# Queries of two heads in one product, moved across partitions by DMA, and the maximum's products of a pair of heads as two row tiles of 64

## The reference, cut to what matters

```
D_MODEL, H, DK, DV = (128, 16, 64, 64)
q = (x @ Wq + bq).reshape(B, S, H, DK)
k = x @ Wk + bk
v = x @ Wv + bv
scores = jnp.einsum('bshd,btd->bhst', q, k) / np.sqrt(DK)
w = jax.nn.softmax(scores, axis=-1)
out = jnp.einsum('bhst,btd->bshd', w, v).reshape(B, S, H * DV)
return out @ Wo + bo
```

## Time and profile before

| | |
|---|---|
| median of three runs | 1417.2 us (1414.25 to 1417.55) |
| the profiled execution | 1409.84 us, span 1408.0 us |
| TensorE busy | 1286.0 us, 91% of the span |
| VectorE busy | 1011.7 us, 72% |
| ScalarE busy | 708.6 us, 50% |
| products for the maximum (L1348) | 512; idle before them 34.9 us |
| reductions for the maximum (L987) | 512 of 685 ns |

### The profile page before, as it was taken

One profiled execution on the slowest core, in us unless ns is written; L12 is line 12 of the kernel. 1 busy time (PEld: TensorE's weight loads), 2 busy tenths in 40 slices (PEclk: granted clock), 3 DMA queues, 4 the chain that ended last, 5 costly groups with the idle time before them and its releaser, 6 DMA issues.

```text
span 1408.0 us, 22235 instructions
## 1 busy us (share of the span) xinstructions
PE 1286.0 (91%) x7377; PEld 760.0 (54%) x7377; DVE 1011.7 (72%) x2393; ACT 708.6 (50%) x1300; POOL 270.9 (19%) x314
## 2 busy tenths in 40 slices
PE   4569988999989998999899999999999979999997
PEld 2335435554545555555454555555655538686844
DVE  7776866578857875787668766876687747677875
ACT  3126544544464445444554445544545448677741
POOL 3033222200120012001200120012000205454630
PEclk9569998999999999999999999999999989999999
DMA  2051433000210021003000200020000246465451
GB/s 75 0 158 61 151 108 138 29 17 19 84 32 17 18 85 32 18 18 85 31 17 19 85 32 17 18 85 32 18 17 19 62 136 207 155 214 170 144 179 48
DMA packets 69299, 100.25 MB, mean 71 GB/s; under 512 B 29196, under 2 KB 45132, under 8 KB 65220
## 3 DMA queue, kind: packets, MB, share of 16 engines
q1 hardware_dynamic: 54628, 66.23, 15.2%
q0 software_dynamic: 11344, 31.64, 6.9%
q10 hardware_dynamic: 3216, 0.97, 0.3%
HBM read 59.86 MB, written 38.68 MB: 70 GB/s over the span
## 4 chain that ended last, share of the span: by engine, by line
PE 73%; DVE 16%; issue 3%; DMA 2%; ACT 2%; SPq 2%; POOL 1%; DVEq 0%; ACTq 0%; POOLq 0%
PE bank L1420 14%; PE bank L1392 8%; PE bank L1348 7%; PE bank L1431 6%; PE bank L1393 6%; PE bank L1256 5%; PE bank L1258 5%; PE bank L1257 5%; PE bank L1452 4%; DVE mneg L987 3%; PE bank L1272 2%; PE bank L1262 2%; DVE q_lm L981 2%; PE bank L1307 2%; PE bank L1289 1%
## 5 line engine op out<-in xcount | busy, mean ns | idle before, releaser
L815 ACT ACTIVATE wide<-bank 128x512 f32<-128x512 f32 x512 | 301.5, 604 | 493.3 <-PE bank L1393 483.0
L987 DVE TENSOR_REDUCE mneg<-bank 128x1 f32<-128x512 f32 x512 | 347.2, 685 | 182.2 <-PE bank L1348 176.5
L1420 PE MATMUL bank<-wide,v_w 128*32 128x512 f32 x2048 | 249.5, 605 | 0.5 <-issue 0.5
L1348 PE MATMUL bank<-k_hl,q_hh 128*128 128x512 f32 x512 | 208.0, 407 | 34.9 <-DVE mneg L987 21.7
L1392 PE MATMUL bank<-q_hh,k_hl 128*128 128x512 f32 x512 | 234.7, 458 | 1.7 <-ACT wide L815 1.4
L1393 PE MATMUL bank<-q_lm,k_h 65*128 65x512 f32 x512 | 203.6, 398 | 0.0
L1392 PEld LDWEIGHTS bank<-q_hh,k_hl 128*128 128x128 f32 x512 | 97.0, 189 | 131.1 <-issue 89.5
L614 POOL TENSOR_TENSOR rs<-rs,power 128x4 f32<-128x4 f32 x24 | 24.6, 1026 | 626.4 <-DVE rs L889 626.4
L1348 PEld LDWEIGHTS bank<-k_hl,q_hh 128*128 128x128 f32 x512 | 98.1, 192 | 72.6 <-issue 51.7
L1431 PE MATMUL bank<-wide,ones 128*32 128x512 f32 x992 | 129.1, 592 | 0.0
L684 POOL DMA_INDIRECT y_rows<-y_m,to_u x92 | 104.2, 1132 | 127.0 <-DVE y_m L1114 105.1
(11 more groups left out here) (231 smaller groups left out, 1970.4 us busy)
## 6 DMA issues: line engine op xcount, KB each, us to landing
w_t<-w_rows SPq DMA_DIRECT2D x23, 1024.0 KB
x_rows<-part_h POOLq DMA_DIRECT2D x65, 258.0 KB, 6.1
inv<-inverse_scratch SPq DMA_DIRECT2D x124, 128.0 KB, 2.9
w_rows<-w_t SPq DMA_DIRECT2D x8, 1024.0 KB, 4.9
x_m<-x_rows SPq DMA_DIRECT2D x23, 258.0 KB, 3.6
stage<-in_L_ffn_W SPq DMA_DIRECT2D x16, 256.0 KB, 5.2
yab<-y_rows POOLq DMA_DIRECT2D x8, 512.0 KB, 9.4
xin<-in_L_attn_x SPq DMA_DIRECT2D x8, 256.0 KB, 5.9
```

Of the source, the lines that this page charges most:

```text
L815: act.activation(wide[:, st.g % WIDE, :], ps, ACT.Exp, scale=SCALE1).then_inc(wide_full, 1)
L987: dve.tensor_reduce(mneg[:, (gh // 2) % 2, col:col + 1], ps[:], X, ALU.max, negate=True)\
L1348: into(("mx", gh, j), lambda ps: pe.matmul(ps[:], q_hh[:, gh % HEADS, P * j:P * j + P], k_hl[:, n % 2, :], start=True, stop=True))
L1420: pe.matmul(ps_out[0][rows, :], v_w[:, n, c, TILE * d:TILE * d + TILE], weights, start=(c == 0), stop=(c == TT - 1))
```

## The change

One product makes the queries of two heads: the weights stand once (`wq_h` of [P, H, DK]), so that the even head's query comes out on partitions 0 to 63 and the odd head's on 64 to 127. ScalarE rounds each half by itself, two activations of 64x512, and two DMAs on SyncE's queue copy each half of `q_hh` to the other 64 partitions, because `first` still wants the query in both halves. VectorE's remainders are two instructions as before, the second with its input on the upper partitions and its output on the lower. The two heads' products for a maximum are issued one behind the other, each of depth 64, with operands on partitions 0 to 63 and 64 to 127, into two banks of the ring. They take rounded keys alone; a new tile `k_hh` holds them on the upper partitions. So the maximum that is subtracted leaves out the keys' remainders. The query of a pair is at s = 2 (two pairs ahead), its `lo_q` at s = 3 ahead of the first layer's pieces, and the products for maxima are at the even places: j = 2 and 3 of the next pair at s = 0 and 2, and j = 0 and 1 of the pair after that at s = 4 and 6.

```
-    LEAD = 3
+    QUERY_AT = 2
-    WO_AT = [ATT - 10, ATT + 17]
+    WO_AT = [ATT - 10, ATT + 18]
...
-        ahead_ = gh + LEAD + s // TT
-        if 0 <= ahead_ < H * NB:
-            events.append(("mx", ahead_, s % TT))
-        if s == TT + 1 and 0 <= gh + 2 < H * NB:
-            events.append(("mt", (gh + 2) // 2))
-        if s % TT == 1 and 0 <= ahead_ + 1 < H * NB:
-            events.append(("q", ahead_ + 1))
+        here, total = gh // 2, H // 2 * NB
+        if s == TT + 1 and 0 <= here + 1 < total:
+            events.append(("mt", here + 1))
+        if s == QUERY_AT and 0 <= here + 2 < total:
+            events.append(("q", here + 2))
+        if s % 2 == 0:
+            pair, j = (here + 1, s // 2 + 2) if s < TT else (here + 2, s // 2 - 2)
+            if 0 <= pair < total:
+                events.append(("mx", pair, j))
...
+            def copy_queries(pair):
+
+                for b in range(2):
+                    gh = 2 * pair + b
+                    here, there = slice(DK * b, DK * b + DK), slice(DK - DK * b, P - DK * b)
+                    sp.wait_ge(qh_done, gh + 1)
+                    sp.dma_start(q_hh[there, gh % HEADS, :].bitcast(F32), q_hh[here, gh % HEADS, :].bitcast(F32))\
+                      .then_inc(q_copied[pair % 2], 16)
...
+            def round_q(pair):
+                ps, _ = filled(act, ("q", pair))
+                for b in range(2):
+                    gh, rows = 2 * pair + b, slice(DK * b, DK * b + DK)
+                    if gh >= HEADS:
+                        act.wait_ge(first_full, last_step(gh - HEADS) + 1)
+                    act.activation(q_hh[rows, gh % HEADS, :], ps[rows, :], ACT.Identity, bias=bq[rows, gh % H:gh % H + 1])\
+                       .then_inc(qh_done, 1)
...
+                    act.activation(k_hh[:, n % 2, :], ps[:], ACT.Identity, bias=bk[:, 0:1])
...
+            def lo_q(pair):
+                ps, free = full(("q", pair))
+                for b in range(2):
+                    gh, rows = 2 * pair + b, slice(DK * b, DK * b + DK)
+                    h, i = gh % H, gh % HEADS
+                    dve.wait_ge(qh_done, gh + 1)
+                    ins = dve.scalar_tensor_tensor(q_lm[0:DK, i, :], ps[rows, :], bq[rows, h:h + 1],
+                                                   q_hh[rows, i, :].bitcast(F32), ALU.add, ALU.subtract)
+                ins.then_inc(free, 1)
+
+            def maximum(pair, j):
+                for b in range(2):
+                    ps, free = full(("mx", 2 * pair + b, j))
+                    col = TT * b + j
+                    dve.tensor_reduce(mneg[:, pair % 2, col:col + 1], ps[:], X, ALU.max, negate=True).then_inc(free, 1)
...
+                pe.wait_ge(qh_done, 2 * pair + 2)
+                for b, keys in enumerate((k_h1, k_hh)):
+                    gh, rows = 2 * pair + b, slice(DK * b, DK * b + DK)
+                    into(("mx", gh, j), lambda ps: pe.matmul(ps[:], q_hh[rows, gh % HEADS, P * j:P * j + P],
+                                                             keys[rows, n % 2, :], start=True, stop=True))
...
+                        if gh % 2 == 0:
+                            read_out(pe, ("q", gh // 2))
+                            pe.wait_ge(q_copied[(gh // 2) % 2], (gh // 4 + 1) * 32)
```

More of the change, by code:

```diff
@@ L211, in head_events, with split_pair, head_uses @@
         gh, events = H * st.r + 2 * p, []
[L212 to L226 removed]
+        here, total = gh // 2, H // 2 * NB
[7 more added lines that the diff above has]
+                events.append(("mx", pair, j))
+        return events
+    def split_pair(st):
+        if st.kind not in ("pre", "o") or st.k % PAIR != QUERY_AT + 1:
+            return None
+        pair = (H * st.r + 2 * (st.k // PAIR)) // 2 + 2
+        return pair if 0 <= pair < H // 2 * NB else None
+    def head_uses(st):
+        return [use for e in head_events(st)
+                for use in ([("mx", 2 * e[1] + b, e[2]) for b in range(2)] if e[0] == "mx" else [e])]
     def wo_at(r, part):
@@ L344, in two_layers @@
         k_hl, k_h1 = sb("k_hl", [P, 2, S], F32R), sb("k_h1", [P, 2, S], F32R)
+        k_hh = sb("k_hh", [P, 2, S], F32R)
         v_w, ones = sb("v_w", [P, 2, TT, DK]), sb("ones", [P, TILE])
@@ L397, in two_layers @@
         m_loaded = [sem(f"m_loaded{i}") for i in range(2)]
+        q_copied = [sem(f"q_copied{i}") for i in range(2)]
         sums_stored, sums_loaded = [sem(f"sums_stored{i}") for i in range(2)], sem("sums_loaded")
@@ L552, in _ @@
             for st in steps:
+                for event in head_events(st):
+                    if event[0] == "q":
+                        copy_queries(event[1])
                 for r, k in row_steps(st):
@@ L632, in _ @@
                 src = raw[:, n, :].rearrange("p (h d) -> p h d", d=DK)
-                for hi, lo in zip(copies(wq_h[:, 8 * n:8 * n + 8]), copies(wq_l[:, 8 * n:8 * n + 8])):
-                    ins = pool.tensor_tensor(lo, src, hi.bitcast(F32), ALU.subtract)
-                ins.then_inc(split_l, 1)
+                pool.tensor_tensor(wq_l[:, 8 * n:8 * n + 8], src, wq_h[:, 8 * n:8 * n + 8].bitcast(F32), ALU.subtract)\
+                    .then_inc(split_l, 1)
             def zero(n):
@@ L802, in _ @@
                         src = raw[:, n, :].rearrange("p (h d) -> p h d", d=DK)
-                        for hi in copies(wq_h[:, 8 * n:8 * n + 8]):
-                            last = act.activation(hi, src, ACT.Identity)
-                        last.then_inc(split_h, 1)
+                        act.activation(wq_h[:, 8 * n:8 * n + 8], src, ACT.Identity).then_inc(split_h, 1)
             act.wait_ge(split_l, 2)
@@ L1207, in _ @@
             for st in steps:
+                if split_pair(st) is not None:
+                    lo_q(split_pair(st))
                 if st.kind in ("pre", "o"):
@@ L1211, in _ @@
                             next(cuts[n], None)
-                if split_head(st) is not None:
-                    lo_q(split_head(st))
                 for event in head_events(st):
@@ L1334, in twice, with query, scores_for_maximum @@
                 return w.rearrange("p t d -> p (t d)")
-            def query(gh):
-                n, h = divmod(gh, H)
+            def query(pair):
+                n, h = divmod(2 * pair, H)
                 if h == 0:
                     read_out(pe, ("xt", n))
[L1340 to L1345, removed]
-                    read_out(pe, ("k", n))
-                pe.wait_ge(qh_done, gh + 1)
-                into(("mx", gh, j), lambda ps: pe.matmul(ps[:], q_hh[:, gh % HEADS, P * j:P * j + P], k_hl[:, n % 2, :],
-                                                         start=True, stop=True))
+                into(("q", pair), lambda ps: three(ps[:], twice(wq_h[:, h:h + 2]), twice(wq_l[:, h:h + 2]),
+                                                   x_h[:, n % 2, :], x_l[:, n % 2, :]))
+            def scores_for_maximum(pair, j):
+                n = 2 * pair // H
+                if 2 * pair % H == 0 and j == 0:
+                    read_out(pe, ("k", n))
+                pe.wait_ge(qh_done, 2 * pair + 2)
[3 more added lines that the diff above has]
+                                                             keys[rows, n % 2, :], start=True, stop=True))
             def turn_maxima(pair):
```

23 lines of the change are left out of this document (2 added, 21 removed).

## The result

The changed kernel takes 1547.8 us (median of 4 runs, 1541.4 to 1550.1) against 1415.7 us: a ratio of 1.093, 95% interval 1.089 to 1.097. I had forecast 1454 us, slower by 2.6%, with a range up to 1488. The direction was right and the size was not: 132 us instead of 37, and outside the range. The ratios of the runs further down are each to the kernel before as it was measured beside that run (1410.7 to 1415.7 us).

The account below looks back on a forecast made before the run. TensorE's program, busy for 91% of the span, was taken as the bound. The profiled 1409.8 us plus 30 over seven samples plus 7 in the last gave 1447; the median's 7.4 made it 1454 us, whole range 1390 to 1488.

Parts of the forecast that it names:

- the last sentence of the prediction: TensorE's granted clock: would be wrong if the 1.9 us waits lowered it, which no equally long earlier wait did.
- The new wait: Second product for a maximum at s = 4 waits for lo_q to free the query's bank: 1.9 us a plain pair.
- The price of a pair of row tiles: Two half-depth products for maxima with their borders: 0.65 us, against 0.47 for the two products replaced; 0.23 from below.
- rival 1: Row tiles for maxima without drain, 0.23 us a pair of tiles instead of 0.65: 1377 us, chance 0.19.
- rival 2: Only one border of the row tiles costs, about 0.42 us a pair of tiles: 1415 us, no change, chance 0.10.
- The sum pair by pair: The eight pairs of a sample, each with its covers and lost waits: +4.2 us a sample, 30 over seven.
- The copies: Two DMA copies of 128 KB a pair, issued at s = 2, asked for over 20 us later: cost nothing.
- Rival 4: The DMA copies arrive late, above all in the last sample, 10 to 30 us in all: 1475 us, chance 0.06.
- Rival 3: Row tiles drain and don't run side by side, 0.23 us more at each pair of tiles: 1483 us, chance 0.11.

Follow-up runs that it names:

- e3: The changed kernel with row tiles and query at s = 2, without the DMA copies (ScalarE writes all 128 partitions of q_hh): 1527.3 us, ratio 1.079.
- e1: The changed kernel with the pair's query one step earlier (s = 1) and lo_q at s = 2; row tiles and copies stay: 1392.3 us, ratio 0.984.
- e5: The changed kernel with the query at s = 1, full-depth products for the maxima and no DMA copies: 1365.4 us, ratio 0.967.
- e8: The changed kernel with the query at s = 1 and its row tiles, without the DMA copies: 1391.1 us, ratio 0.982.
- e9: The changed kernel with its copies, row tiles and query at s = 2, but ScalarE writing all 128 partitions and VectorE's wait changed: 1523.4 us, ratio 1.081.
- e2: The changed kernel with full-depth products for the maxima, without the DMA copies; query at s = 2 and its wait stay: 1471.8 us, ratio 1.041.
- e11: The changed kernel with query at s = 1, one rounded tile for both heads, full-depth products with zero-padded keys, four copies a pair: 1374.5 us, ratio 0.972.
- e7: The kernel before with one head's lo_q behind the reduction of s = 4 in pairs p = 1, 3, 4, last sample excepted: 1430.2 us, ratio 1.011.
- e10: The changed kernel with lo_q at s = 2 ahead of the step's two reductions, nothing else: 1477.6 us, ratio 1.047.

## Why the prediction was wrong, and where it was right

1. **The step that failed** is the last sentence of the prediction, and with it the clock's place in the sum: that waits of 1.9 us don't bring the clock down because those of the earlier trace rows didn't, so that a new wait costs its own length alone. The runs showed instead that the waits took TensorE to half clock, 186 us more of half-clock time, some 87 of the 132 us. "As long as that" was wrong too: the longest wait of the earlier trace rows is 1.36 us, and the new one was to be 1.9. I read the clock from the page's slices, each 35 us wide, where a short stretch at half clock still shows as 9. The windows of 2 us around the longest wait of before (the 1.36 us ahead of 532.32) say otherwise:

```profile
530.00:532.00 2.00, 0.48 (x1) 0.19 (x1) 1.93 (x4) 1.88 (x2) 0.00 (x0) 1.00 0.50 170
532.00:534.00 2.00, 1.68 (x2) 0.68 (x3) 1.90 (x7) 0.00 (x0) 0.00 (x0) 0.62 0.29 92
534.00:536.00 2.00, 2.00 (x4) 0.96 (x3) 1.90 (x5) 0.73 (x2) 0.00 (x0) 0.52 0.00 0
536.00:538.00 2.00, 2.00 (x8) 1.23 (x8) 0.40 (x2) 1.77 (x3) 0.00 (x0) 1.00 0.00 0
```

The evidence was there, in part. Of the kernel before's 18 waits of 1.1 to 1.4 us between 230 and 1070 us, four have such a stretch beside them, and all four are among the six in front of L1272. The same wait one sample earlier (ahead of 390.11) has none, nor has any of the six waits of 1.35 us in front of L1348, such as the one ahead of 475.50:

```profile
390.00:392.00 2.00, 1.89 (x4) 0.68 (x4) 1.86 (x8) 0.69 (x1) 0.00 (x0) 1.00 0.23 65
...
476.00:478.00 2.00, 2.00 (x19) 0.69 (x21) 1.85 (x6) 1.12 (x3) 0.00 (x0) 1.00 0.00 0
```

I named the clock only among the things that would make the prediction wrong, with no price and no chance. It should have been a rival: 50 waits, each with a stretch that costs about 1.6 us, is at most 80 us on top of 1454, 1534 us; how many would have one, the trace of before couldn't tell. Pairs of one p differ only by such a stretch: in e3 the pair p = 1 took 15.4 us in one sample and 16.9 to 17.0 in the others; the difference over the length of the stretch at half clock, 3.4 us, is 0.47. The half-clock time grew by 186 us, which at 0.47 is 87 of the 132 us (an estimate, from one kind of pair).

The Trainium skill, "TensorE: Matmul & The Clock Gate", The HAM clock gate, names two levels and lets activity release the throttle; the trace shows both levels and the fall behind idle time. Its section on HAM oscillation has the clock fall in waits for DMA that are longer than the 1.3 to 1.5 us in front of L1373, beside which it fell here 22 times of 26; the measurement decides.

2. **The new wait** was right in place, cause and size: the ring's fifth use, `lo_q` behind two reductions, 1.8 us for 1.9 from start to start. What I called its idle time, 1.9 us, was 1.3 to 1.5 by the profile, and so 57.5 us in all and not 80. e1 removes it by its cause.

3. **The price of a pair of row tiles** was right as a time (1.08 us for 1.1 in the timeline), and that they run side by side too. The choice of 0.65 over 0.23, by the way into and out of the column tiles, held: rival 1, which ends at 1377 us, did not come, and no more did rival 2. Where nothing waits they cost 26 us (e5 to e8), against 0.15 x 256 = 38 by the timeline. The rule that a change of the tiling mode drains TensorE ("TensorEngine Tiling (Array Packing)", Key Properties) agrees with the trace: 0.32 us into the tiles (460.68 to 461.00), 0.42 out of them (461.00 to 461.42) and 0.34 to the next product (461.42 to 461.76), where 0.23 is the pace of full products.

4. **The sum pair by pair**, from one `first` of s = 0 to the next. Without a stretch at half clock, p = 1 grew by 1.5 us (15.37 in e3 against 13.85), as worked out, p = 2 shrank by 0.4, as worked out, p = 6 grew by 1.4, and p = 0 by 0.9 for 0.55. There TensorE waits 1.8 us a sample for ScalarE's `v`, which stands behind the two roundings of the query, a wait that my sum doesn't name:

```profile
PE bank L1284 <- ACT v L744: 12.3, 7, 1.8
```

But p = 4 grew by 1.4 with the wait of 1.35 at its start counted as gone: it had only moved to the turns of the first layer's tiles, in the kernel after:

```profile
PE bank L1351 <- DVE mneg L1010: 10.3, 7, 2.0
```

p = 7 kept its length, to some 0.3 us, where I had 1.4 us less: the wait before the first layer's products grew, from 9.5 us in all to

```profile
PE bank L1294 <- DVE q_lm L1002: 21.6, 7, 4.5
```

Together some 6.7 us a sample instead of 4.2, 18 us over seven samples. By the pairs the steps' own part of the loss is so 37 + 18 = 55 us; by the clock it is what is left, 132 - 87 = 45. The two counts are 10 us apart, and I can't say which is nearer; by both the clock has the larger part.

5. **The copies**, which I put at nothing, cost nothing (e8, e9). They land 2.6 us after the issue:

```profile
q_hh<-q_hh SPq DMA_DIRECT2D x128, 128.0 KB, 2.6
```

Rival 4 is out. Rival 3 is out by the common start at 461.00.

What stays open: why some waits have a stretch of half clock beside them and others of the same length have none, why a wait among row tiles costs more of the clock than the same wait among full products (71 us more of half-clock time in e3 than in e2), and the 1.1 points between the kernel after and e9.

## What to carry to other kernels

Before taking work out of a TensorE-bound program, write down its timetable with the rings' order: the wait was predictable to 0.1 us, and moving one query by one step was worth 156 us. Then price the clock: a new wait of more than a microsecond on a dense TensorE can cost its length a second time, as four of 18 did before and 22 of 26 for `lo_q` after. Whether one does is looked up with windows of 2 us around the waits that are there already, not with the page's wide slices. Two half-depth products need not be row tiles: with zeros in the other half of the moving operand both stay full-depth products (e11).

## What the runs showed of the hardware

- In the kernel after, 22 of 26 waits of 1.3 to 1.5 us between matmuls, in a stream that is dense otherwise, had a stretch of half clock beside them that began between 0.9 us before the wait's end and 1.8 us after it. One of them cost 1.7 us in the work behind it. Waits of 0.8 us in three pairs of a sample had none (e7); of e10's waits of 0.4 us among row tiles, 8 of 21 had one.
- Two float32r products of depth 64 on partitions 0 to 63 and 64 to 127 start together, and cost 0.15 us more with their borders than two full-depth ones.
- Row tiles and waits together lowered the clock more than the sum of both: 152 us of half-clock time from e5 to e3, where the tiles alone brought 13 and the waits alone 81.
